# Attention sums in two channel halves, with the order of all engines written anew

## The reference

```python
h = group_norm(x, gn_w, gn_b)
q, k, v = conv1x1(h, wq, bq), conv1x1(h, wk, bk), conv1x1(h, wv, bv)
w = softmax(einsum('bcq,bck->bqk', q, k) * C ** -0.5)
x1 = x + conv1x1(einsum('bqk,bck->bcq', w, v), wo, bo)

att = einsum('bcn,bdn->bcd', x1, x1)
feat_e = einsum('bcd,bdn->bcn', softmax(max(att) - att), x1)
fb, fc, fd = conv1x1(x1, wb, bb), conv1x1(x1, wc, bc), conv1x1(x1, wd, bd)
att_s = softmax(einsum('bkn,bkm->bnm', fb, fc))
feat_p = einsum('bcm,bnm->bcn', fd, att_s)
out = (beta * feat_e + x1) + (alpha * feat_p + x1)
```

## Time and profile before

| what | value |
|---|---|
| timed runs | 431.71, 431.94, 432.14 us; median 431.94 |
| profiled execution | 434.71 us, of which the profile's span 432.8 |
| TensorE matmuls | busy 414.9 us (96%), 2090 instructions |
| TensorE weight loads | 282.2 us (65%), beside the matmuls |
| VectorE | 308.0 us (71%), 476 instructions |
| ScalarE | 242.5 us (56%), 324 instructions |
| GpSimd | 53.8 us (12%) |
| mean granted TensorE clock | 0.993 |
| DMA | 48.02 MB moved, 36.52 of them on the transposes' queue; HBM read 9.90 MB, written 4.19 |
| DMA transpose | 64, median 4.4 us from issue to landing |

### The profile page before, as it was taken

How to read it: one execution, slowest core, us unless ns; L and a number is a source line. 1 busy time by engine, 2 the same in 40 slices (tenths; PEclk the granted TensorE clock), 3 DMA queues, 4 the chain that set the end, 5 groups by cost and what they waited for, 6 DMA issues and landing times.

```text
span 432.8 us, 5686 instructions
## 1 busy us (share of the span) xinstructions
PE 414.9 (96%) x2090; PEld 282.2 (65%) x2090; DVE 308.0 (71%) x476; ACT 242.5 (56%) x324; POOL 53.8 (12%) x51
## 2 busy tenths in 40 slices
...
GB/s 236 133 160 91 92 87 218 72 123 2 0 123 73 105 237 145 102 96 48 122 220 48 78 119 177 115 97 2 0 142 151 145 120 78 97 145 130 163 98 48
DMA packets 140395, 48.02 MB, mean 111 GB/s; under 512 B 135824, under 2 KB 137296, under 8 KB 140368
## 3 DMA queue, kind: packets, MB, share of 16 engines
q1 hardware_dynamic: 136400, 36.52, 45.1%
...
HBM read 9.90 MB, written 4.19 MB: 33 GB/s over the span
## 4 chain that ended last, share of the span: by engine, by line
PE 87%; DMA 4%; DVE 3%; ACT 3%; issue 2%; SPq 0%; POOLq 0%; POOL 0%; ACTq 0%; DVEq 0%
PE sum_ps L814 13%; PE sum_ps L815 13%; PE sum_ps L816 13%; PE score_ps L814 13%; PE score_ps L816 12%; PE score_ps L815 12%; PE score_ps L968 3%; PE score_ps L939 3%; DMA x<-in_x_dram 2%; DMA x<-in_L_conv_wo_dram 2%; PE score_ps L949 2%; ACT exps L432 1%; PE score_ps L824 1%; DVE g_l L540 1%; PE score_ps L976 1%
## 5 line engine op out<-in xcount | busy, mean ns | idle before, releaser
L432 ACT ACTIVATE exps<-score_ps,negmax 128x1024 f32<-128x1024 f32 x64 | 71.2, 1113 | 73.6 <-DVE negmax L673 56.8
L689 DVE SCALAR_TENSOR_TENSOR pieces<-exps,recip,pieces 128x1024 f16<-128x1024 f32 x64 | 87.0, 1366 | 19.6 <-ACT pieces L442 19.4
L673 DVE TENSOR_REDUCE negmax<-score_ps 128x1 f32<-128x1024 f32 x64 | 77.6, 1217 | 16.5 <-PE score_ps L816 13.0
L442 ACT ACTIVATE pieces<-exps,recip 128x1024 f16<-128x1024 f32 x64 | 72.4, 1142 | 20.0 <-DMA land<-pieces 11.3
L814 PE MATMUL score_ps<-xn_h,g_h 128*128 128x512 f32 x128 | 53.4, 417 | 1.1 <-DVE fd_l L712 0.7
L815 PE MATMUL score_ps<-xn_l,g_h 128*128 128x512 f32 x128 | 50.7, 396 | 0.0
L816 PE MATMUL score_ps<-xn_h,g_l 128*128 128x512 f32 x128 | 50.6, 396 | 0.0
L814 PE MATMUL sum_ps<-land,fd_h 128*128 128x512 f16 x128 | 48.8, 381 | 0.0
L814 PE MATMUL sum_ps<-land,v_h 128*128 128x512 f16 x128 | 48.8, 381 | 0.0
L815 PE MATMUL sum_ps<-land,fd_h 128*128 128x512 f16 x128 | 48.5, 379 | 0.0
L816 PE MATMUL sum_ps<-land,fd_l 128*128 128x512 f16 x128 | 48.5, 379 | 0.0
...
## 6 DMA issues: line engine op xcount, KB each, us to landing
...
land<-pieces SPq DMA_TRANSPOSE x64, 4.4
...
```

The lines of the kernel that those rows point to most:

```text
L432: act.activation(exps[:, n % 2, :], score_ps[s][:, :], ACT.Exp, bias=negmax[:, n % RING:n % RING + 1], scale=1.0, accum_out=rowsum[:, n % ...
L442: act.activation(pieces[:, n % 2, 0, :], exps[:, n % 2, :], ACT.Copy, scale=recip[:, n % RING:n % RING + 1]).then_inc(high_piece, 1)
L673: dve.tensor_reduce(negmax[:, n % RING:n % RING + 1], score_ps[s][:, :], AX.X, ALU.max, negate=True)\
L689: dve.scalar_tensor_tensor(pieces[:, n % 2, 1, :], exps[:, n % 2, :], recip[:, n % RING:n % RING + 1], pieces[:, n % 2, 0, :], ALU.mult, A ...
```

## The change

In `sum_steps` the loop over the halves is now outside and the loop over the slabs inside. All eight slabs of half 0 are added first, then all eight of half 1, and one step is two slabs of one half (still six products). The number of steps of each sum stays. The wait for the emptied bank of a sum of block 0 now stands at the start of each half, and the waits for the two halves of V or FD stand at slabs 0 and 4 of half 0 only. Half 0 is thus complete after step 4 of 8 (block 0) or step 6 of 10 (block 2).

```diff
-                for t in range(NT):
-                    if t % 4 == 0:
-                        done(f"FD.{b}.{t // 4}" if block_no else f"V.{b}.{t // 4}")
-                    for m in range(CH):
-                        if block_no == 0 and t == 0:
-                            if k:
-                                pe.wait_ge(sum_done[m], k)
-                            else:
-                                pe.wait_ge(scale_made, 1)
+                for m in range(CH):
+                    if block_no == 0 and k:
+                        pe.wait_ge(sum_done[m], k)
+                    elif block_no == 0 and m == 0:
+                        pe.wait_ge(scale_made, 1)
+                    for t in range(NT):
+                        if m == 0 and t % 4 == 0:
+                            done(f"FD.{b}.{t // 4}" if block_no else f"V.{b}.{t // 4}")
                         last = product(sum_ps[m][:, :], both(v, every, t, cols(m)),
                                        [land[:, k % HALVES, piece, t, :] for piece in range(2)],
                                        block_no == 0 and t == 0, t == NT - 1)
                         if t == NT - 1:
                             last.then_inc(sum1_full if m else sum0_full, 1)
-                    yield
+                        if t % 2:
+                            yield
```

All four lists of steps are written anew. They hold the same steps with the same names. In PE_ORDER few places differ: MEAN.3 goes behind S0.2.3 and a step of O2.0.1 from behind XT.1.1 to before G.2.1; S2.1.2 goes two steps of O0.2.0 up and AT.1 down; near the end steps of O2.2.1 move behind S2.3.4 and S2.3.7 goes up before all steps of O2.3.0:

```diff
-    S2.0.6 O2.0.0x3 S0.2.0 S2.0.7 O0.1.1x4 S0.2.1 XT.1.0 O0.1.1x4 FBC.1.0 MEAN.3 S0.2.2 O2.0.1x2 S0.2.3 O2.0.1x1
-    G.2.1 O2.0.1x1 XT.1.1 O2.0.1x1 FBC.1.1 O2.0.1x1 ATT.1 MX.1 O2.0.1x1 S2.1.0 O2.0.1x1 S2.1.1 S0.2.4 O2.0.1x1
-    V.2.0 S0.2.5 O2.0.1x1 V.2.1 FD.1.0 O0.2.0x3 AT.1 S2.1.2 S2.1.3 O0.2.0x5 VAR.3 S2.1.4 FD.1.1 S0.2.6 ET.1
-    AT.3 O2.2.0x3 S2.3.2 O2.2.1x2 MX.3 FD.3.0 S2.3.3 O2.2.1x3 ET.3 S2.3.4 S2.3.5 O2.2.1x3 S2.3.6 O2.2.1x2 FD.3.1
-    O2.3.0x4 S2.3.7 O2.3.0x6 O2.3.1x10
+    S2.0.6 O2.0.0x3 S0.2.0 S2.0.7 O0.1.1x4 S0.2.1 XT.1.0 O0.1.1x4 FBC.1.0 S0.2.2 O2.0.1x2 S0.2.3 MEAN.3 O2.0.1x2
+    G.2.1 O2.0.1x1 XT.1.1 FBC.1.1 O2.0.1x1 ATT.1 MX.1 O2.0.1x1 S2.1.0 O2.0.1x1 S2.1.1 S0.2.4 O2.0.1x1 V.2.0
+    S0.2.5 O2.0.1x1 V.2.1 FD.1.0 O0.2.0x1 S2.1.2 O0.2.0x2 AT.1 S2.1.3 O0.2.0x5 VAR.3 S2.1.4 FD.1.1 S0.2.6 ET.1
+    AT.3 O2.2.0x3 S2.3.2 O2.2.1x2 MX.3 FD.3.0 S2.3.3 O2.2.1x3 ET.3 S2.3.4 O2.2.1x1 S2.3.5 O2.2.1x2 S2.3.6
+    O2.2.1x2 FD.3.1 S2.3.7 O2.3.0x10 O2.3.1x10
```

In ACT_ORDER and DVE_ORDER the places that the text below speaks of are these. `fx` and `fo` of half 0 stand apart from those of half 1 and earlier everywhere, for example:

```diff
-    hFD.1.0 xb.2.0 xb.2.1 exp2.1.2 exp2.1.3 expE.1 a2.1.2 a2.1.3 exp2.1.4 hFD.1.1 hET.1 exp0.2.6 xnh.3.0 xnh.3.1
-    hXT.2.1 base.2.0 base.2.1 exp0.3.4 a0.3.4 cA.2 exp0.3.5 a0.3.5 expE.2 exp0.3.6 ldx1.3 a0.3.6 exp0.3.7 xb.3.0
-    exp2.2.0 a0.3.7 hET.2 xb.3.1 exp2.2.1 a2.2.0 exp2.2.2 a2.2.1 hFD.2.0 x1h.3.0 exp2.2.3 a2.2.2 hXT.3.0
-    exp2.2.4 a2.2.3 exp2.2.5 a2.2.4 x1h.3.1 hFD.2.1 a2.2.5 exp2.2.6 exp2.2.7 hXT.3.1 hFBC.3.0 a2.2.6 a2.2.7
-    hFBC.3.1 base.3.0 cA.3 base.3.1 exp2.3.0 exp2.3.1 a2.3.0 expE.3 a2.3.1 exp2.3.2 hFD.3.0 a2.3.2 exp2.3.3
+    hFD.1.0 exp2.1.2 xb.2.0 xb.2.1 exp2.1.3 a2.1.2 expE.1 a2.1.3 exp2.1.4 hFD.1.1 hET.1 exp0.2.6 xnh.3.0 xnh.3.1
+    hXT.2.1 base.2.0 base.2.1 exp0.3.4 a0.3.4 cA.2 exp0.3.5 a0.3.5 expE.2 ldx1.3 exp0.3.6 a0.3.6 xb.3.0 exp0.3.7
+    xb.3.1 exp2.2.0 a0.3.7 hET.2 a2.2.0 exp2.2.1 exp2.2.2 x1h.3.0 hFD.2.0 a2.2.1 a2.2.2 exp2.2.3 exp2.2.4
+    hXT.3.0 a2.2.3 exp2.2.5 a2.2.4 x1h.3.1 hFD.2.1 exp2.2.6 a2.2.5 hXT.3.1 base.3.0 exp2.2.7 hFBC.3.0 a2.2.6
+    hFBC.3.1 a2.2.7 cA.3 base.3.1 exp2.3.0 exp2.3.1 a2.3.0 expE.3 a2.3.1 exp2.3.2 hFD.3.0 a2.3.2 exp2.3.3 hET.3
...
-    r2.1.1 max0.2.4 b2.1.0 b2.1.1 r0.2.4 lV.2.0 max0.2.5 fo.0.1.0 fo.0.1.1 b0.2.4 r0.2.5 lV.2.1 b0.2.5 lFD.1.0
-    aA.1 max2.1.2 max2.1.3 minE.1 r2.1.2 r2.1.3 nE.1 b2.1.2 gvar.3 max2.1.4 fx.2.0.0 fx.2.0.1 b2.1.3 lFD.1.1
-    max0.2.6 lET.1 xn.3.0 xn.3.1 r2.1.4 max0.2.7 r0.2.6 b2.1.4 b0.2.6 max2.1.5 r0.2.7 r2.1.5 max2.1.6 b0.2.7
-    lG.3.1 lFBC.2.1 lV.3.1 lXT.2.1 max0.3.4 r0.3.4 b0.3.4 sA.2 max0.3.5 fo.1.1.1 fo.1.1.0 aA.2 r0.3.5 minE.2
-    lFBC.3.0 b2.2.6 b2.2.7 lFBC.3.1 sA.3 max2.3.0 max2.3.1 aA.3 r2.3.0 minE.3 r2.3.1 fo.2.0.0 fo.2.0.1 b2.3.0
-    max2.3.6 r2.3.5 b2.3.4 fo.2.1.0 fo.2.1.1 r2.3.6 b2.3.5 lFD.3.1 b2.3.6 max2.3.7 r2.3.7 b2.3.7 fo.3.0.0
+    r2.1.1 max0.2.4 b2.1.0 b2.1.1 r0.2.4 lV.2.0 max0.2.5 fo.0.1.1 b0.2.4 r0.2.5 lV.2.1 b0.2.5 lFD.1.0 max2.1.2
+    aA.1 max2.1.3 r2.1.2 minE.1 fx.2.0.0 r2.1.3 b2.1.2 nE.1 gvar.3 max2.1.4 fx.2.0.1 b2.1.3 xn.3.0 lFD.1.1
+    max0.2.6 lET.1 xn.3.1 r2.1.4 max0.2.7 r0.2.6 b2.1.4 b0.2.6 max2.1.5 r0.2.7 r2.1.5 max2.1.6 b0.2.7 lG.3.0
+    max0.3.2 lFBC.2.0 fx.2.1.0 b0.3.1 r0.3.2 max0.3.3 b0.3.2 r0.3.3 fx.2.1.1 mx.2 b0.3.3 lV.3.0 sF.2 fo.1.1.0
+    lG.3.1 lFBC.2.1 lV.3.1 lXT.2.1 max0.3.4 r0.3.4 b0.3.4 sA.2 max0.3.5 fo.1.1.1 aA.2 r0.3.5 minE.2 max0.3.6
+    lFBC.3.0 b2.2.6 lFBC.3.1 b2.2.7 sA.3 max2.3.0 max2.3.1 aA.3 r2.3.0 minE.3 r2.3.1 fo.2.0.1 b2.3.0 max2.3.2
+    max2.3.6 r2.3.5 b2.3.4 fo.2.1.1 r2.3.6 max2.3.7 b2.3.5 lFD.3.1 r2.3.7 b2.3.6 fo.3.0.0 b2.3.7 fo.3.0.1
```

More of the change, by code:

```diff
@@ L43 @@
     hG.1.1 hFBC.0.1 hXT.0.0 exp2.0.0 exp2.0.1 hFD.0.0 hXT.0.1 a2.0.0 a2.0.1 base.0.0 base.0.1 exp2.0.2 cA.0
[L44 to L47, removed]
@@ L53 @@
-    exp2.2.4 a2.2.3 exp2.2.5 a2.2.4 x1h.3.1 hFD.2.1 a2.2.5 exp2.2.6 exp2.2.7 hXT.3.1 hFBC.3.0 a2.2.6 a2.2.7
-    hFBC.3.1 base.3.0 cA.3 base.3.1 exp2.3.0 exp2.3.1 a2.3.0 expE.3 a2.3.1 exp2.3.2 hFD.3.0 a2.3.2 exp2.3.3
-    hET.3 a2.3.3 exp2.3.4 exp2.3.5 a2.3.4 exp2.3.6 a2.3.5 hFD.3.1 a2.3.6 exp2.3.7 a2.3.7
+    a2.0.2 exp2.0.3 expE.0 hFD.0.1 a2.0.3 exp0.1.4 hET.0 exp0.1.5 a0.1.4 xnh.2.0 exp0.1.6 xnh.2.1 a0.1.5 x1h.1.0
+    a0.1.6 exp0.1.7 exp2.0.4 a0.1.7 hG.2.0 exp2.0.5 a2.0.4 exp2.0.6 a2.0.5 exp0.2.0 a2.0.6 exp2.0.7 a0.2.0
```

39 lines of the change are left out of this document (21 added, 18 removed).

## The result

The change made the kernel slower. Four timed runs had a median of 438.86 us (435.36 to 440.05) against 432.04 us (431.71 to 433.13) for the kernel before on the same chip: ratio 1.0121, 95% interval 1.0073 to 1.0168. The same code timed twelve times on another occasion stood at 1.0043 [1.0011, 1.0075]. It is slower both times, by an amount that spreads. The forecast was 430.0 us, with 0.10 for slower. Ratios and their intervals leave out every run over 1.5% above the fastest of its kernel (none of these four, four of the twelve), be it disturbed or slow by a long wait of its own, and medians keep all, so where the two differ the ratio is the low figure for a loss.

A forecast was written before the change was run, and what follows sets the result against it. TensorE, busy 96% of the span, was taken as the bound, so only gaps and the tail could move. Terms -0.5 - 0.7 - 0.7 - 0.8 + 0.8 = -1.9 us, off the 431.94 median, gave 430.0 us; 8-in-10 range 428.6 to 431.9.

The forecast's parts named there:

- part 3: New order around 330 us: image 3's load lands sooner, but xb.3.0 waits ahead of exp0.3.7; net -0.8 us.
- O2.3.1's gap: Wait at 413 us for fo.3.0.0, forecast to go because half 0 is done earlier: -0.5 us.
- the tail: After the last product only one update and one store remain instead of two each: -0.7 us (0.5 to 0.85).
- S0.2.7: Step near 237 us waiting for the slot lFD.1.1 empties, forecast to start sooner: -0.7 us, bounds 0 and -0.8.
- AT.3: Step near 374 us needing sA.3's slot, forecast to start later under the new order at 362 to 374: +0.8 us.
- part 2: New order around 237 us: exp2.1.2 fills ScalarE's idle stretch, so S0.2.7 starts sooner; -0.7 us.
- the store's landing: Near 320 us: O2.1.1's last store, issued at 317.2, lands in 2.7 us, so image 3's load goes at 320.0.
- a head start: Image 3's load issues 1.7 us sooner, ahead of S0.3.5's transpose, and so takes 6.7 us instead of 8.4.
- L - 327.5: Change in FD.2.0's start near 336 us, with L the landing of image 3's load; not under -1.9 us.
- Rival C: Slower: xb.3.0 waits at the queue's head for a load landing at 329.3; sum +0.7 us, 432.6 us; chance 0.12.
- ET.2 at L + 2.4: Near 330 us: ET.2 starts 2.4 us after image 3's load lands (L), for xb 1.1 and exp 1.2.
- TensorE hides them: Other rearranged places (176 to 195 us, 140 us, swaps) cost nothing; ATT.1 closest, slipping 0.1 to 0.3 us if at all.

The follow-up runs named there:

- e9: The kernel before with the new half-by-half sum loops and the changed kernel's order in the last stage only: 432.26 us, ratio 0.9973 to the kernel before.
- e1: The kernel before with only the new half-by-half sum loops, all engine orders as before: 435.07 us, ratio 1.0030 to the kernel before.
- e4: The kernel before with one swap on ScalarE, xb.3.0 ahead of exp0.3.7: 437.52 us, ratio 1.0051 to the kernel before.
- e5: The changed kernel again without any edit, timed beside its repairs: 435.88 us, ratio 1.0043 to the kernel before.
- e6: The changed kernel with one swap on GpSimd, st.0.0.1 ahead of st.0.0.0: 438.73 us, ratio 1.0030 to the kernel before.

## Why the prediction was wrong

In the profile the span went up by 5.4 us where 1.9 less was forecast, 7.3 apart: part 3 is off by 5.0, two gaps that were put at nothing by 2.9, and the other terms take back some 0.6.

**Right.** The products of the sums keep their rate (same 379 ns; e9). O2.3.1's gap went (-0.5 forecast, -0.7 measured), the tail gave -0.85 for -0.7, S0.2.7 -0.83 for -0.7, AT.3 +1.0 for +0.8. Together these four terms were forecast at -1.1 and came to -1.4. With S0.2.7 there is luck in it: its gap of 0.7 us was that of one execution. Under the same order of these steps it was 0.2 in e1 and e4 and nothing in e9, so what part 2 can be counted on for is less than its term. A slip without effect: the products of the sums and the scores are 1152 of 1520 with 512 columns, three quarters and not two thirds.

**Part 3 failed in its first step, the store's landing.** I gave the single store the 2.7 us of the first of a pair. It was issued when I said (317.2 once the 1.73 us by which the trace was late there are taken off), but took 4.4 us, and the load went at 321.60 on that scale and not at 320.0: 0.1 sooner than the 321.73 of before. In all ten profiles with the store alone at this place it took 3.7 to 4.7 us; in the four with a pair the first took 2.3 to 2.7 and the second 3.9 to 4.1. The row to take was the pair's second. It is not that a lone store is slow: the two lone stores of 370 to 390 us, in the profile after, landed in 2.3.

```profile
DMA to landing us min/median/max: 2.3/2.3/2.3
```

What is different at 319 is a packet of instruction fetch (below). The next step, landed 6.7 us after the issue, leaned on a head start that wasn't there: 8.9 us here, and 5.4 in e5. With L at 330.5 on that scale my own term L - 327.5 says +3.0.

**Rival C was the mechanism, and its price was too low.** It put L at 329.3, and what stood against it was that "the store must land no sooner or the load be slower than it ever was". The store landed no sooner, and the load took 8.5 us beside the 8.0 of before. The rule ET.2 at L + 2.4 held to 0.01 us. The rest of the +4.2 is the clock, 1.5 us behind the gap, which stood in no case, less 0.4 by which my stretch from ET.2 to FD.2.0 (6.3 us, 5.95 in e5) was too long. I gave C 0.12 although the argument had one measured sample of this load, 8.4 us, and a hope why it would be shorter. That sample could have come out either way: over 14 profiles the second half took 4.9 to 8.5 us. The head start would have mattered more than I said: in the four profiles where the second half of the load was issued ahead of the transpose of that moment it took 4.9 to 5.2 us, in the ten where the transpose went first 5.5 to 8.5.

**"TensorE hides them" was false in two places.** The sentence on the other rearranged places allowed ATT.1 0.1 to 0.3; it was 1.1, because I followed the instructions moved next to ATT.1 and not the 2.28 us of mx.1, at the head of a chain of six: b, transpose, a, hG, hXT, lXT. And O0.1.1 (+1.8) I never priced. The halves were credited with early updates and stores, but what an early store meets on the DMA engines was worked out for 320 us only, not for 151, where a load and a transpose already shared them. The rule I weighed there (the Trainium skill, DMA: Bandwidth & Descriptors, "Issuing engines are not separate DMA queues") held at exactly the place that I didn't apply it to: the transpose went from 7.6 to 10.0 us beside a third transfer, of which e6, without that transfer, takes 1.8 back. The mark that I set myself, a gap over 0.3 us in 31 to 225, is met twice.

**Open.** Why the same load takes 5.5 us in one execution and 8.5 in the next when the transpose went first in both; who goes first was not set by a run either. What each of the repairs at O0.1.1, ATT.1 and AT.3 is worth alone: their gaps are shown closed, their times don't separate. And 0.3% of e1, whose interval begins at 1.0000: the 0.9 us wait in its last sum is only a part of it.
